# Projections one step sooner, batch loops written out, score rows split around the attend products

## The chip, the cores and the metric

The kernel runs on one core of one Trainium2 chip. The metric is the device time of one execution in microseconds (us). The engines of the core are named as the profile names them: PE (TensorE, with its weight loads as PEld), DVE (VectorE), ACT (ScalarE), POOL (GpSimd) and SP (SyncE, which issues the DMA transfers here). They run side by side, each through its own list of instructions, and meet at semaphores.

## The reference, cut to what matters

Two blocks are computed for x of 4 batches, 512 tokens and 512 columns. The first normalises each token, sends it through one of four experts and adds the gated result. The second, which the change touches, is this for each batch:

```python
def _L0_ffn_ref(hidden_states, ln1_w, ln2_w, Wq, Wk, Wv, Wo, A, B, W_in_base, W_up_base, W_down):
    ...   # H = 16 heads of HD = 32 columns, F_ = 2048, R = 16
    residual = hidden_states
    x = _rmsnorm(hidden_states, ln1_w)
    attn = _attention(x, Wq, Wk, Wv, Wo)      # causal softmax attention
    mod = MOD_SCALE * jnp.tanh(attn @ A)
    h = _rmsnorm(residual, ln2_w)
    gate_pre = h @ W_in_base.T + mod * (h @ A) @ B
    gate = jax.nn.silu(gate_pre)
    up = h @ W_up_base.T
    mlp_out = gate * up @ W_down.T
    return residual + mlp_out
...
x = x + jnp.tanh(g_ffn[0]) * _L0_ffn_ref(_layernorm(x, axis=-1), ...)
```

## The kernel before

All products keep single-precision accuracy by splitting an operand into a high and a low part (fp32r). The high part is an ACT copy, the low part a DVE subtraction, and a product of two split operands is three matmuls. The expert part runs first, to about 161 us. Then the four batches follow, each with an attention stage and an MLP stage of 16 chunks. On every engine but POOL the batches 0 to 2 are one loop (`Fori(0, NB - 1)`, on SP `Fori(1, NB - 1)`) and the last is written behind it.

The attention stage has 16 heads in four groups of four. For each group a Q and a K product (12 matmuls each) go to one PSUM bank, `QKB`, which holds one product at a time: the next may start once ACT has copied the high part (`split_qk`) and DVE has taken the low part (`qk_low`) of the one before. SP loads each head's rows of Q and K into one of two stacks (`load_stack`, three transfers). For head n the steps are then:

- scores (PE, `scores`): four row tiles of 512, 384, 256 and 128 columns, in three banks. The widest one (bank 0) is followed by its causal mask, an added product with the identity; then the 384 and 128 tiles share bank 1 and one mask; then 256 in bank 2 with its mask. Each bank must have been read by the exponentials of the head before.
- maxima (DVE, `maxima`), exponentials (ACT, `exponentials`, four of them, each with its row sum), the reciprocal of the sums (DVE) and the normalisation of the four tiles: `NORM_DVE` tiles 3 and 1 on DVE, `NORM_POOL` tiles 0 and 2 on POOL.
- turn (PE, `turn_probs`): ten transposes of 128x128 into the banks 4, 5 and 6, each of which must be free of the head before; ACT copies the high parts and DVE subtracts the low parts (three each) into `pts`.
- attend (PE, `attend`): eight matmuls against the values, all heads into the one bank `ATT`, which a product with zeros has cleared.

The engines overlap these steps for neighbouring heads. PE's order is written out by hand in `head_step`: in step n it does half a Q or K product if one is due (6 matmuls), the turn of head n+1, the scores of head n+3, the attend products of head n, and in the steps 9 to 14 two matmuls of the first chunk's up product (`up_part`). ACT's step n is the exponentials of n+1, a Q/K copy or a copy of values if due, and the three copies of head n. DVE's step n is reciprocal and normalisation of n+1, a Q/K low part if due, the maxima of n+2, and the three low parts of n. The half products stand in the steps 0 to 8.

## Time and profile before

| | us |
|---|---|
| median of 3 runs | 1061.95 (1060.31 to 1062.95) |
| the profiled execution, its own time | 1061.96 |
| its span (first to last instruction) | 1059.8 |
| PE busy / DVE / ACT / POOL in the span | 1033.5 / 722.4 / 589.6 / 252.1 |

The profiled execution stands for the median: they differ by 0.01 us, and 2.2 us of its time lie around the span. A stage is read by cutting the span where PE changes work. The second batch serves as the example: its opening products begin at 385.40, its first scores at 396.80, the attend products of head 0 at 411.53, of head 7 at 444.23, the first product of the MLP stage at 475.63. The clock of PE is granted in full throughout.

### The profile page before, as it was taken

How to read it: one execution, taken by the hardware profiler on the slowest of the kernel's cores; microseconds unless marked ns; L12 is line 12 of the kernel's file. 1: busy time of each engine (PE TensorE's matmuls, PEld its weight loads, DVE VectorE, ACT ScalarE, POOL GpSimd, SP SyncE). 2: the span in 40 equal slices, each digit the busy share in tenths (PEclk: the TensorE clock that was granted, in tenths of full speed). 3: DMA queues.
4: the chain of work that ended last, by engine and by line, in shares of the span. 5: the costliest groups of instructions: out<-in, count | busy, mean ns of one | idle time of the engine just before them, and what ended most of it. 6: DMA issues, size and time to landing. Idle time of an engine off the chain costs nothing.

```text
span 1059.8 us, 17623 instructions
## 1 busy us (share of the span) xinstructions
PE 1033.5 (98%) x5336; PEld 853.5 (81%) x5337; DVE 722.4 (68%) x1661; ACT 589.6 (56%) x1399; POOL 252.1 (24%) x252
## 2 busy tenths in 40 slices
PE   6999999999999999999999999999999999999998
PEld 6787878877888878878888888778888888788887
DVE  7766756996665559985665479966655599854443
ACT  4464546886434447875444368864344478753342
POOL 4536123641000115640000136410001155300000
PEclk9999999999999999999999999999999999999999
DMA  6534133443222416343322354432234253322221
GB/s 239 201 141 161 49 117 74 96 110 134 90 89 91 147 47 173 69 127 129 106 90 89 111 141 98 113 130 90 89 91 147 63 157 80 95 86 89 89 89 50
DMA packets 47084, 115.93 MB, mean 109 GB/s; under 512 B 6800, under 2 KB 6800, under 8 KB 46096
## 3 DMA queue, kind: packets, MB, share of 16 engines
q1 hardware_dynamic: 43968, 105.06, 33.2%
q0 software_dynamic: 3040, 9.96, 2.7%
q8 instruction: 35, 0.57, 0.2%
q14 instruction: 41, 0.34, 0.1%
HBM read 76.46 MB, written 13.37 MB: 85 GB/s over the span
## 4 chain that ended last, share of the span: by engine, by line
PE 86%; DVE 8%; issue 3%; DMA 1%; ACT 1%; SPq 0%; DVEq 0%; POOL 0%; POOLq 0%
PE bank L518 67%; PE bank L721 5%; PE bank L735 4%; DVE wr L1329 3%; PE bank L684 3%; DVE nb L1341 2%; PE bank L688 1%; PE bank L770 1%; DMA stack<-wr 1%; PE bank L574 1%; PE bank L589 1%; DVE big L1350 1%; PE bank L632 1%; SPq L312 0%; ACT wr L887 0%
## 5 line engine op out<-in xcount | busy, mean ns | idle before, releaser
L518 PE MATMUL bank<-hT,wr 128*128 128x512 f32 x1488 | 358.4, 390 | 0.0
L518 PEld LDWEIGHTS bank<-hT,wr 128*128 128x128 f32 x1488 | 278.8, 188 | 60.0 <-issue 1.3
L518 PE MATMUL bank<-wr,actr 128*128 128x512 f32 (+1 forms) x1224 | 303.1, 397 | 2.4 <-DVE actr L1311 1.5
L518 PEld LDWEIGHTS bank<-wr,actr 128*128 128x128 f32 x1224 | 228.8, 190 | 51.1 <-issue 3.3
L491 POOL TENSOR_SCALAR big<-big,rr 128x128 f32<-128x128 f32 (+1 forms) x128 | 138.9, 1094 | 131.7 <-DVE rr L1346 131.2
L1380 DVE SCALAR_TENSOR_TENSOR wr<-stream,lns,wr 128x256 fp32r<-128x256 f32 x256 | 121.7, 536 | 51.0 <-ACT wr L1006 51.0
L972 ACT ACTIVATE big<-bank,nb 128x512 f32<-128x512 f32 (+3 forms) x256 | 131.7, 527 | 27.9 <-DVE nb L1341 27.7
L430 POOL TENSOR_TENSOR wqs<-wstage,wqs 128x512 fp32r<-128x512 f32 x32 | 43.0, 1353 | 436.8 <-ACT wqs L887 435.4
L1329 DVE TENSOR_TENSOR wr<-bank,wr 128x512 fp32r<-128x512 f32 (+1 forms) x224 | 124.5, 600 | 22.2 <-ACT wr L887 22.2
L887 ACT ACTIVATE wr<-bank 128x512 fp32r<-128x512 f32 (+1 forms) x224 | 106.0, 538 | 52.9 <-PE bank L518 30.1
L887 ACT ACTIVATE actr<-act_sb 128x512 fp32r<-128x512 f32 x64 | 40.4, 632 | 145.7 <-DVE act_sb L1394 145.7
L1018 ACT ACTIVATE sil<-bank 128x512 f32<-128x512 f32 x64 | 38.1, 596 | 137.3 <-PE bank L770 137.3
L1341 DVE TENSOR_REDUCE nb<-bank 128x1 f32<-128x512 f32 (+3 forms) x256 | 107.2, 478 | 3.7 <-PE bank L688 3.0
L1006 ACT ACTIVATE wr<-stream,lns 128x256 fp32r<-128x256 f32 x256 | 108.4, 494 | 0.0
L518 PE MATMUL bank<-hT,wqs 128*128 128x512 f32 x384 | 98.2, 398 | 2.2 <-issue 2.2
L1329 DVE TENSOR_TENSOR wr<-stream,wr 128x512 fp32r<-128x512 f32 x64 | 43.8, 690 | 72.4 <-ACT wr L887 71.7
L721 PE MATMUL bank<-ident,big 128*128 128x128 f32 x640 | 84.9, 276 | 6.0 <-DVE wr L1329 5.0
L721 PEld LDWEIGHTS bank<-ident,big 128*128 128x128 f32 x640 | 71.3, 140 | 23.7 <-DVE wr L1329 14.0
L735 PE MATMUL bank<-wr 128*48 128x512 f32 (+3 forms) x512 | 86.0, 310 | 0.0
L1394 DVE TENSOR_TENSOR act_sb<-bank,sil 128x512 f32<-128x512 f32 x64 | 44.2, 691 | 57.7 <-PE bank L518 51.0
L518 PEld LDWEIGHTS bank<-hT,wqs 128*128 128x128 f32 x384 | 68.8, 188 | 16.3 <-issue 3.9
L735 PEld LDWEIGHTS bank<-wr 128*48 128x48 f32 x512 | 58.2, 122 | 22.9 <-DVE wr L1329 1.8
(180 smaller groups left out, 1039.6 us busy)
## 6 DMA issues: line engine op xcount, KB each, us to landing
stream<-in_wmlp SPq DMA_DIRECT2D x64, 512.0 KB, 4.0
stack<-wr SPq DMA_DIRECT2D x192, 128.0 KB, 2.3
stream<-in_wmlp SPq DMA_DIRECT2D x64, 256.0 KB, 2.7
big<-in_x SPq DMA_DIRECT2D x4, 1024.0 KB
big<-y_rows SPq DMA_DIRECT2D x4, 1024.0 KB, 5.5
residual<-big SPq DMA_DIRECT2D x4, 1024.0 KB
big<-residual SPq DMA_DIRECT2D x4, 1024.0 KB, 5.6
out<-big SPq DMA_DIRECT2D x3, 1024.0 KB, 4.5
```

What stands on the lines that cost most here:

```text
L430: g.tensor_tensor(wqs[:, LO, which, :, :], wqk_v[:, which, :, q * P:q * P + P], wqs[:, HI, which, :, :].bitcast(F32), ALU.subtract).then_i ...
L491: g.tensor_scalar(rows, rows, rr[:, n % 2, qt:qt + 1], None, ALU.mult).then_inc(pn_pool, 1)
L518: mm = pe.matmul(dst, lhs(pl, k), rhs(pr, k), start=start and i == 0, stop=stop and i == n - 1, skip_group_check=skip)
L721: mm = pe.transpose(bank[bk][:, col + (qt - kt) * P:col + (qt - kt) * P + P], prob[par][:, src:src + P], ident[:, :])
L735: mm = pe.matmul(bank[ATT][0:3 * R, kt * P:S], vst[:, q % 2, kt, at_row:at_row + 3 * R], pts[:, j % 2, part, at:at + w], start=False, stop ...
L887: return a.activation(dst, src, ACT.Copy)
L972: a.activation(prob[par][:, at:at + w], bank[bk][:, col:col + w], ACT.Exp, bias=nb[:, qt:qt + 1], accum_out=rs[:, par, qt:qt + 1]).then_in ...
L1006: ins = a.activation(dst[:, :, dt, :], raw[:, :, dt, :], ACT.Copy, scale=lns[:, 1, dt:dt + 1])
L1329: v.tensor_tensor(dst, src, high.bitcast(F32), ALU.subtract).then_inc(done, 1)
L1341: v.reduce_max(nb[:, qt:qt + 1], bank[bk][:, col:col + P * (qt + 1)], AXX, negate=True).then_inc(nb_ok, 1)
L1380: ins = v.scalar_tensor_tensor(out=dst[:, :, dt, :], in0=raw[:, :, dt, :], scalar=lns[:, 1, dt:dt + 1], in1=high[:, :, dt, :].bitcast(F32) ...
L1394: v.tensor_tensor(act_sb[:, :], bank[UP[par]][:, :], sil[:, :], ALU.mult).then_inc(gu_ok, 1)
```

## The change

The Q and K products of the groups 2 and 3 move one step forward: half a product stands at the end of the steps 0 to 6, in front of these one half stands behind the scores of head 2, and the second half of group 1's K product joins the first, ahead of the first turn. So the steps 7 and 8 have none. Their copies (`COPY_AT`) and POOL's weight splits (`WEIGHTS_AT`) move with them. In PE's step n the turn comes first, then the middle and the second bank of the scores of head n+3, then the attend products of head n, then the half product or the up products, then the first (widest) score tile of head n+4. The turn takes the key tiles in another order, and so the three banks are copied smallest first; the attend products wait once for all three banks. Normalisation is shared out anew: tile 3 on DVE, tile 0 on ACT behind its first copy, tiles 1 and 2 on POOL. ACT copies the values ahead of the three copies. The product with zeros is gone, the first attend product starts the bank. The batch loops of PE and SP are written out; those of ACT and DVE stay. The value products use their two banks in the other order.

```diff
-VALUES, LOW_RANK = (4, 6), 5
+VALUES, LOW_RANK = (6, 4), 5
-NORM_DVE, NORM_POOL = (3, 1), (0, 2)
+NORM_DVE, NORM_ACT, NORM_POOL = 3, 0, (1, 2)
+TURN_ORDER = (2, 1, 3, 0)
+TURNED_BANKS = ((6, 256, 1024), (5, 512, 512), (4, 512, 0))
+COPY_AT = {(0, 0): (1, 1), (0, 2): (2, 0), (1, 0): (2, 1), (1, 2): (3, 0), (2, 0): (3, 1)}
+WEIGHTS_AT = {(0, 0): (2, 1), (0, 2): (3, 0), (1, 0): (3, 1)}
+PART_OF = {2: 1, 1: 2, 3: 2, 0: 3}
...
@@ SP: load_stack, batch loop
                     sp.wait_ge(qk_lo, g * 2 + 2)
+                    if q:
+                        sp.wait_ge(s_done, g * (3 * QH) - 3)
...
-            batch(0, True, first=True)
-            with sp.Fori(1, NB - 1) as b:
-                batch(b, True)
-            batch(NB - 1, False)
+            for b in range(NB):
+                batch(b, b < NB - 1, first=b == 0)
...
@@ PE
-            def scores(n, par, loads, first=False):
...
+            def scores_last(n, par, loads, first=False):
                 pe.wait_ge(stk[par], loads)
                 if not first:
                     pe.wait_ge(exp_ok, n * 4 - 3)
+                score_rows(par, 3, True)
                 mask(0, 3 * P, 1)
+            def scores_middle(n, par, first=False):
                 if not first:
                     pe.wait_ge(exp_ok, n * 4 - 1)
+                score_rows(par, 2, True)
+                score_rows(par, 0, False)
                 mask(1, 2 * P, 2)
+            def scores_second(n, par, first=False):
                 if not first:
                     pe.wait_ge(exp_ok, n * 4)
+                score_rows(par, 1, True)
                 mask(2, P, 1)
...
+            def turn_tiles(n, par, kt, first=False):
+                if not first and kt != 3:
+                    pe.wait_ge(pt_lo, (n - 1) * 3 + PART_OF[kt])
+                for qt in range(kt, TT):
+                    turn(n, par, kt, qt)
+            def wait_probs(n):
+                pe.wait_ge(pn_ok, n + 1)
+                pe.wait_ge(pn_act, n + 1)
+                pe.wait_ge(pn_pool, (n + 1) * len(NORM_POOL))
+            def project_part(b, head):
+                q, j = head // QH, head % QH
+                if q < NQ - 2:
+                    project(b, q + 2, j // 2, half=j % 2)
+            def head_step(b, q, j):
+                n = (b * NQ + q) * QH + j
+                head, other = q * QH + j, (j + 1) % 2
...
+                if head < H - 1:
+                    wait_probs(n + 1)
+                    for kt in TURN_ORDER:
+                        turn_tiles(n + 1, other, kt)
+                if head < H - 3:
+                    scores_middle(n + 3, other)
+                    scores_second(n + 3, other)
+                order = (0, 1, 3, 2) if head < H - 1 else TURN_ORDER
+                for i, kt in enumerate(order):
+                    if head == H - 1 and kt != 3:
+                        pe.wait_ge(pt_lo, n * 3 + PART_OF[kt])
+                    elif i == 0:
+                        pe.wait_ge(pt_lo, n * 3 + 3)
+                    attend(kt, HI)
+                    mm = attend(kt, LO)
                 mm.then_inc(pv_done, 1)
                 if head < H - 1:
-                    turn_probs(n + 1, (j + 1) % 2)
...
+                    project_part(b, head + 1)
                 if UP_FROM <= head < H - 1:
...
+                if head < H - 4:
+                    scores_last(n + 4, j % 2, stack_loads(b, head + 4))
...
+                pe.wait_ge(qk_lo, b * (NQ * 2) + 1)
                 values((0, 1))
-                pe.matmul(bank[ATT][:, :], zeror[:, :], hT[:, HI, 0, :], start=True, stop=False,
-                          skip_group_check=True).then_inc(pv_done, 1)
                 pe.wait_ge(qk_lo, b * (NQ * 2) + 2)
+                scores(b * H, 0, stack_loads(b, 0), first=True)
                 project(b, 1, 0)
+                scores(b * H + 1, 1, stack_loads(b, 1))
                 values((2, 3))
+                project(b, 1, 1)
+                wait_probs(b * H)
...
+                scores(b * H + 2, 0, stack_loads(b, 2))
+                project_part(b, 0)
+                scores_last(b * H + 3, 1, stack_loads(b, 3))
...
-            with pe.Fori(0, NB - 1) as b:
-                batch(b, True)
-            batch(NB - 1, False)
+            for b in range(NB):
+                batch(b, b < NB - 1)
@@ ACT
+            def normalise(n, par):
+                act.wait_ge(rr_ok, n + 1)
+                rows = prob_rows(par, NORM_ACT)
+                a.activation(rows, rows, ACT.Copy, scale=rr[:, par, NORM_ACT:NORM_ACT + 1]).then_inc(pn_act, 1)
...
+                for i, (bk, w, at) in enumerate(TURNED_BANKS):
+                    act.wait_ge(p_turned, n * 3 + i + 1)
+                    copy(pts[:, j % 2, HI, at:at + w], bank[bk][:, 0:w]).then_inc(pt_hi, 1)
+                    if i == 0 and (q < NQ - 1 or j < QH - 1):
+                        normalise(n + 1, (j + 1) % 2)
...
@@ DVE
-                for qt in NORM_DVE:
-                    rows = prob_rows(par, qt)
-                    v.tensor_scalar(rows, rows, rr[:, par, qt:qt + 1], None, ALU.mult).then_inc(pn_ok, 1)
+                rows = prob_rows(par, NORM_DVE)
+                v.tensor_scalar(rows, rows, rr[:, par, NORM_DVE:NORM_DVE + 1], None, ALU.mult).then_inc(pn_ok, 1)
...
```

## Rows read from the trace of the kernel before

**Rows 1.** The page: busy time and share of the span, per engine.
```profile
PE 1033.5 (98%) x5336; PEld 853.5 (81%) x5337; DVE 722.4 (68%) x1661; ACT 589.6 (56%) x1399; POOL 252.1 (24%) x252
```

**Rows 2.** Windows of the second batch's attention stage: start:end, length, each engine's busy us.
```profile
396.80:411.53 14.73, 14.73 (x97) 13.38 (x97) 13.98 (x37) 11.57 (x36) 7.59 (x8) 1.00 0.74 216
444.23:475.63 31.40, 29.96 (x198) 22.62 (x197) 29.49 (x70) 24.79 (x73) 13.88 (x13) 1.00 0.37 95
444.23:448.88 4.65, 4.65 (x33) 3.97 (x33) 4.62 (x12) 3.98 (x12) 2.56 (x3) 1.00 0.00 0
461.94:466.09 4.15, 4.10 (x29) 3.11 (x29) 4.12 (x11) 3.62 (x11) 2.18 (x3) 1.00 0.69 244
```

**Rows 3.** Timeline of PE: start, us, line, operation; one step with half a product.
```profile
444.23 1.34 PE L735 MATMUL bank<-wr 128*48 128x512 f32 x8
445.41 1.60 PE L518 MATMUL bank<-hT,wqs 128*128 128x512 f32 x6
446.85 1.25 PE L721 MATMUL bank<-ident,big 128*128 128x128 f32 x10
447.86 0.47 PE L684 MATMUL bank<-stack 96*128 96x512 f32 x1
...
448.23 0.45 PE L684 MATMUL bank<-stack 96*128 96x384 f32 x2
...
```

**Rows 4.** Timeline of PE: turns of later heads; idle time before one, and its releaser.
```profile
450.82 1.47 PE L721 MATMUL bank<-ident,big 128*128 128x128 f32 x10 [0.60 <-DVE wr L1329]
...
463.84 1.47 PE L721 MATMUL bank<-ident,big 128*128 128x128 f32 x10
```

**Rows 5.** Timeline of DVE: a reciprocal with products about, then one later step.
```profile
442.66 0.16 DVE L1346 RECIPROCAL rr<-rs 128x4 f32<-128x4 f32 x1
...
460.49 0.16 DVE L1346 RECIPROCAL rr<-rs 128x4 f32<-128x4 f32 x1
460.69 0.86 DVE L1350 TENSOR_SCALAR big<-big,rr 128x512 f32<-128x512 f32 x2
461.50 1.68 DVE L1341 TENSOR_REDUCE nb<-bank 128x1 f32<-128x512 f32 x4
463.10 1.61 DVE L1329 TENSOR_TENSOR wr<-bank,wr 128x512 fp32r<-128x512 f32 x3
```

**Rows 6.** Timeline of ACT, one later step: first and last exponential piece, copies.
```profile
462.23 0.69 ACT L972 ACTIVATE big<-bank,nb 128x512 f32<-128x512 f32 x1 [0.37 <-DVE nb L1341]
...
464.16 0.21 ACT L972 ACTIVATION_READ_ACCUMULATOR big<-bank,nb 128x1 f32 x1
464.53 1.47 ACT L887 ACTIVATE wr<-bank 128x512 fp32r<-128x512 f32 x3 [0.16 <-PE bank L721]
```

**Rows 7.** Groups by shape: count, busy us, mean ns of one, idle before.
```profile
L491 POOL TENSOR_SCALAR big<-big,rr 128x384 f32<-128x384 f32 x64 | 79.5, 1242 | 0.0
L491 POOL TENSOR_SCALAR big<-big,rr 128x128 f32<-128x128 f32 x64 | 60.6, 947 | 131.7 <-DVE rr L1346 131.2
...
L1350 DVE TENSOR_SCALAR big<-big,rr 128x512 f32<-128x512 f32 x64 | 31.1, 486 | 2.3
...
L972 ACT ACTIVATE big<-bank,nb 128x128 f32<-128x128 f32 x64 | 23.4, 366 | 0.0
...
L887 ACT ACTIVATE wr<-bank 128x512 fp32r<-128x512 f32 x160 | 88.3, 597 | 52.9 <-PE bank L518 30.1 <-PE bank L721 19.7 <-DMA stack<-wr 3.1
```

**Rows 8.** Windows over the seams of batches 0/1, 1/2, 2/3: same work, three times.
```profile
381.70:391.62 9.92, 8.85 (x39) 6.69 (x38) 4.71 (x7) 3.12 (x7) 0.00 (x0) 1.00 0.03 8
606.79:616.74 9.95, 8.84 (x40) 6.69 (x37) 4.71 (x7) 3.12 (x7) 0.00 (x0) 1.00 0.03 8
832.07:840.33 8.26, 8.26 (x39) 6.85 (x38) 4.70 (x7) 3.13 (x7) 0.00 (x0) 1.00 0.01 3
```

**Rows 9.** Timeline of PE: behind the first seam, and a batch's first scores.
```profile
171.72 0.50 PE L684 MATMUL bank<-stack 96*128 96x512 f32 x1 [0.26 <-DMA stack<-wr]
...
385.40 2.56 PE L518 MATMUL bank<-hT,wqs 128*128 128x512 f32 x10 [0.72 <-issue]
```

More of the change, by code:

```diff
@@ L745, in head_step, with attend @@
[L745 to L748 removed]
+                head, other = q * QH + j, (j + 1) % 2
+                def attend(kt, part):
+                    _, _, at = TURNED[kt]
+                    at_row = 64 * (j // 2) + R * (j % 2)
+                    return pe.matmul(bank[ATT][0:3 * R, kt * P:S], vst[:, q % 2, kt, at_row:at_row + 3 * R],
+                                     pts[:, j % 2, part, at:at + S - kt * P], start=head == 0 and kt == 0 and part == HI, stop=False,
+                                     skip_group_check=True)
```

111 lines of the change are left out of this document (43 added, 68 removed).

## The prediction, made before the changed kernel had run

> **What bounds the kernel now.** The page comes first: PE is busy for 98% of the span [rows 1]. That seems to leave 26 us, but busy is not the same as useful, so the stage that the change touches is cut into windows next. In the second batch the attention stage, from its first scores at 396.80 to the MLP stage at 475.63, has two different halves. While half products are in the steps, PE is busy without a gap, 4.65 us a step [rows 2]. In the later steps, such as the one from 461.94, DVE is busy for 4.12 of 4.15 us, and PE does not need that long [rows 2]. What PE needs is read from starts on its timeline [rows 3]: attend 445.41 - 444.23 = 1.18, half product 446.85 - 445.41 = 1.44 (six matmuls of 512 columns, 0.24 each), turn 447.86 - 446.85 = 1.01, widest score tile with mask 0.37, the other score tiles 448.88 - 448.23 = 0.65. Together 4.65, the whole step. Without the half product it is 3.21, with two up matmuls (0.48) 3.69; the rest of the later steps' 4.15 is DVE's pace. The trace says so too: the turn at 450.82 comes 0.60 late because of DVE, and the turn, 1.25 long in a full step, is drawn out to 1.47 there [rows 3, 4]. DVE's own step is reciprocal to next reciprocal: 0.20 + 0.81 + 1.60 + 1.53 = 4.14 by its starts [rows 5]. A third loss lies between the batches: the same opening work takes 9.92 and 9.95 us where the batch loop of PE jumps back, and 8.26 us at the last batch, which is entered without a jump [rows 8]. PE stands there with nothing to wait for (0.72 at 385.40 put down to issue [rows 9]).
>
> **The seams.** Writing PE's loop out makes the first two seams like the third: 9.92 + 9.95 - 2 x 8.26 = 3.35 us gained, with no loss elsewhere that the trace suggests, since the straight code behind the third seam runs without gaps. Loops of ACT and DVE stay, but both wait for PE at the seam. From the trace alone the gain lies between 0 (PE must fetch the same instructions either way, rival 2) and 3.35; I take 3.3.
>
> **The opening up to the first attend.** It took 396.80 to 411.53, 14.73 us, all busy [rows 2]. One half product more stands here: +1.44. The turn of head 1 follows sooner behind the scores of head 2, whose maxima DVE has to do before the low parts of head 0; laid out from the durations of rows 3 to 7, PE waits 0.3 there (0 to 0.5). Sum +1.7 a batch. The product with zeros (0.24) gives nothing: the first scores behind it wait for the stack's load [rows 9], and that load starts when K is split, which is not moved. The weights (POOL), the copies of Q and K and the stacks of this part all end before PE wants them, by 0.6 us or more in the same layout; SP's added wait asks for scores that are done one step before.
>
> **The steps with half products.** From the attend of head 0 to that of head 7 the stage took 444.23 - 411.53 = 32.70 [rows 2]; seven steps of 4.65 are 32.55, so 0.2 of small waits goes. What changes inside a step are neighbours. The trace shows 0.07 us of excess where the 512 tile and its mask (640 columns, 0.30 at the pace of the half product) follow the turn, 0.37 [rows 3]; that tile now follows a half product. In exchange a turn now follows a 128-column mask, which the trace of before never shows, and the 384 tile follows the turn. I take 0 for the exchange; bounds -0.10 (the excess is all lost with the old neighbours) and +0.05 a step (it moves to the new ones and the mask hides less of the turn's first weights). Over 12 steps and 4 batches: -4.8 to +2.4 us.
>
> **The steps without.** From the attend of head 7 to the MLP stage the stage took 31.40, PE idle for 1.44 of it and stretched for more [rows 2]. PE's own work there is after the change: 2 x 3.21 (steps 7 and 8 have no filler), 3 x 3.69, 2 x 2.66 (attend, up, turn, no scores left), 1.66, and the last attend 1.20: 25.7. Whether PE reaches that is decided by the others. DVE loses one normalisation of 256 columns: the pair takes 0.86, the 512 tile alone 0.49 [rows 5, 7], so 4.14 - 0.38 = 3.76 a step. ACT's step was 464.37 - 462.23 = 2.14 for the exponentials and 1.36 to 1.47 for the copies [rows 6]; it gains a normalisation of 128 columns. No such ACT row exists; the exponential of 128 columns takes 0.37 [rows 7], and overlapped starts cost about 0.1 less, so I take 0.25 (bounds 0.2 and 0.6, the latter if it also waits for the reciprocal, which DVE issues after the exponentials and its own low parts). ACT's step is then 3.80. POOL's two tiles are 256 and 384 columns where they were 128 and 384: 0.95 and 1.24 [rows 7] give 1.10 for 256 on the straight line, 2.34 in sum, far below 3.8, but it stands between reciprocal and turn.
>
> So ACT and DVE do a step in 3.8, PE in 3.2 to 3.7, and PE lives on a **lead** that the others have built: turn of a head minus its reciprocal. It was 446.85 - 442.66 = 4.2 with products about and 463.84 - 460.49 = 3.35 where DVE binds [rows 3 to 5]. After the change the others need some 4.15 in a full step (3.8, plus a Q/K part every other step, a value copy every fourth), PE 4.65, so the lead grows by 0.5 a step up to what the scores allow: the reciprocal of head n+2 comes at least 1.65 of PE work (turn and two score groups) and about 1.3 (last maximum, last exponential, hand-over) behind the start of the turn of n, so the lead is at most 2 x 4.65 - 2.95 = 6.35. I take 5.9 at head 8. From the turn of head 8 to that of 15 PE needs 23.5 (2 x 3.21 + 3 x 3.69 + 3.3 + 2.7), the reciprocals 7 x 3.8 + 0.85 (one Q/K part, one value part) = 27.5, and the last turn can't start before its reciprocal plus 2.65 (POOL's 2.34 and two hand-overs). PE waits 27.5 + 2.65 - 23.5 - 5.9 = 0.75, bounds 0 and 2.5 (a lead of 4.2). So 25.7 + 0.7 = 26.4 in place of 31.4: -5.0 a batch.
>
> POOL's tiles can be counted in another way. The 128-column tile takes 0.95 and one three times as wide 1.24 [rows 7], so some of the first is waiting beside DVE's normalisation, which starts with it. The Trainium skill ("SBUF — State Buffer", section "Who interferes with whom") says that a VectorE `tensor_scalar` in a two-port mode takes a port pair which GpSimd shares, and that the second to come is blocked until the first ends. By that rule the columns alone would cost 1.24/384 x 256 = 0.83 and the wait 0.43 behind a shorter DVE operation, 2.5 in place of 2.34 for both, and the sum below would be 0.6 us higher.
>
> **The sum.** A batch: +1.7 - 0.2 - 5.0 = -3.5. Four batches and the seams: -14.0 - 3.3 = -17.3. Against the profiled execution's 1061.96, which stands for the median of 1061.95, that is 1044.7. The MLP stages, where PE is the bound, and the expert part are untouched. Unknowns: exchange of neighbours -4.8 to +2.4, waits at the end of the stage -3.0 to +7.2, wait at head 1 -1.2 to +0.8: from 1036 to 1055.
>
> **Rivals.** (1) *ACT takes DVE's place*, 15%. If the normalisation in front of ACT's last two copies costs 0.55 or more with its wait, ACT's step is 4.14 again, DVE's old pace. Then the lead stays at 4.2, the reciprocals take 29.8, and PE waits 29.8 + 2.65 - 23.5 - 4.2 = 4.75 a batch: 4.0 worse than the forecast, a batch no longer gains, and with the seams 1044.7 + 16.0 = 1060.7 is left. For it: ACT is strictly in order and the reciprocal is waited for in the middle of its copies. Against: ACT had 0.53 us idle a step where DVE was the bound [rows 6], and the reciprocal follows the exponentials within 0.3.
>
> (2) *The written-out loop doesn't do what it says*: the seam is instruction fetch that straight code pays elsewhere, 15%. Then 1044.7 + 3.3 = 1048.0. Against it stands the third seam.
>
> (3) *The bank of Q and K becomes the new wait*, 8%, the side where it gets slower. Half products stand directly behind the attend products now, and the first half of each product waits until ACT (0.60 [rows 7]) and DVE (about as much) have split the one before, which they do behind the exponentials and the normalisation of the next step. By my layout the split is done about 1 us ahead of PE at the step with the smallest lead, and later by more. If it came after PE by w at the three products of a batch that start in the steps 1, 3 and 5, it would cost 12 w, and behind it on PE stand the next score tile and the next turn. From w = 1.45 it eats the whole gain; if the split falls one set of exponentials further back (w = 2.3 by 2.14 of rows 6), the time is 1044.7 + 27.6 = 1072.3. For it: before, the copies had a full step more. Against: a wait on PE gives the others lead, so that it should not repeat.
>
> **How the numbers follow.** Forecast 62%, rivals 15, 15 and 8%. A measurement of this kernel can tell about 0.3% (3.2 us) from no change. Faster by more: the forecast, rival 2 and a third of rival 1, 82%. Within: two thirds of rival 1 and the mild end of rival 3, 12%. Slower: 6%. The forecast's own range is 1036 to 1055; rival 2 lies in it, and with it the range holds a little under 8 in 10, so it reaches to 1057, into rival 1.
>
> **What would show it.** Right: no issue gaps at the three seams; steps of heads 1 to 7 at 4.65; the steps behind at 3.2 to 3.7 with PE idle under 1 us a batch; DVE idle for 5 to 10% there; the attend of head 0 about 1.7 later behind the first scores. Wrong: later steps at 4.1 with ACT without a gap (rival 1), a gap in front of half products released by DVE (rival 3), issue gaps inside the stage (rival 2), full steps of 4.7 or more (the exchange of neighbours). A stack that lands late, or POOL, would show as the releaser of the turn or of the widest tile.

## The result, and the profile after

The changed kernel takes **1054.3 us** (median, 1053.1 to 1055.7) where the kernel before takes 1061.35 (1060.3 to 1063.0) beside it: a ratio of 0.9927, 95% interval 0.9914 to 0.9940. The spans of the two profiled executions are 1053.2 and 1059.8 us. So it is 7 us faster; the forecast was 17 us.

The windows answer to [rows 2, 8]: the first two seams between batches, and in the second batch the opening (first scores to the attend of head 0), the steps with half products (to the attend of head 7) and the later steps (to the MLP stage). After start:end come the length, then the busy us of PE, PEld, DVE, ACT and POOL, the clock, DMA share and GB/s.

```profile
381.25:389.51 8.26, 8.26 (x39) 6.85 (x38) 4.71 (x7) 3.13 (x7) 0.00 (x0) 1.00 0.01 4
394.78:412.15 17.37, 16.17 (x102) 14.34 (x103) 13.50 (x33) 11.96 (x39) 10.19 (x10) 1.00 0.72 205
412.15:443.93 31.78, 31.78 (x220) 27.39 (x219) 29.53 (x69) 28.46 (x91) 20.94 (x19) 1.00 0.39 88
443.93:472.52 28.59, 27.93 (x191) 21.15 (x191) 26.64 (x63) 25.25 (x79) 15.36 (x13) 1.00 0.40 102
603.59:611.85 8.26, 8.26 (x40) 6.85 (x39) 4.71 (x7) 3.13 (x7) 0.00 (x0) 1.00 0.02 6
```

Against the forecast, per batch: opening 17.37 - 14.73 = **+2.64** (forecast +1.7), steps with half products 31.78 - 32.70 = **-0.92** (-0.2), later steps 28.59 - 31.40 = **-2.81** (-5.0). Together -1.09 where -3.5 was forecast. The seams give 9.92 + 9.95 - 2 x 8.26 = 3.35, as forecast. With four batches that is 7.7, near the 6.6 and 7.05 of spans and medians. The second batch stands for the others: by PE's timeline the later steps of the four are 28.59, 28.59, 28.94 and 28.57 (one step of the third is 0.34 longer), the other stretches agree within 0.02.

PE's timeline shows the opening's loss: the turn of head 1 starts 1.20 late, put down to a low part of DVE. Behind the dots stand an attend near the end of the batch (L764) and the last turn of the batch, which comes 0.52 late for POOL.

```profile
408.99 0.23 PE L692 MATMUL bank<-maskr,identr 128*128 128x128 f32 x1
410.42 1.31 PE L727 MATMUL bank<-ident,big 128*128 128x128 f32 x10 [1.20 <-DVE wr L1374]
...
466.19 1.42 PE L764 MATMUL bank<-wr 128*48 128x512 f32 x8
468.60 1.28 PE L727 MATMUL bank<-ident,big 128*128 128x128 f32 x10 [0.52 <-POOL big L497]
```

DVE's timeline names the low part (409.95, taken from SBUF, not from a bank: it is that of the values). It also shows a step with half products that has a hole in front of the maxima (439.40) and a later step that has none (446.49 to 450.26: 0.20 + 0.41 + 1.64 + 1.52 = 3.77; 4.14 before, [rows 5]).

```profile
409.95 0.41 DVE L1374 TENSOR_TENSOR wr<-big,wr 128x256 fp32r<-128x256 f32 x1
...
437.87 0.17 DVE L1391 RECIPROCAL rr<-rs 128x4 f32<-128x4 f32 x1
...
439.40 1.09 DVE L1386 TENSOR_REDUCE nb<-bank 128x1 f32<-128x384 f32 x3 [0.24 <-PE bank L692]
...
446.49 0.17 DVE L1391 RECIPROCAL rr<-rs 128x4 f32<-128x4 f32 x1
446.69 0.48 DVE L1394 TENSOR_SCALAR big<-big,rr 128x512 f32<-128x512 f32 x1
447.10 1.73 DVE L1386 TENSOR_REDUCE nb<-bank 128x1 f32<-128x512 f32 x4
448.74 1.61 DVE L1374 TENSOR_TENSOR wr<-bank,wr 128x256 fp32r<-128x256 f32 x3
450.26 0.17 DVE L1391 RECIPROCAL rr<-rs 128x4 f32<-128x4 f32 x1
```

The lead of head 8 (start of its turn on PE minus its reciprocal on DVE) is 442.23 - 437.87 = 4.36, where the forecast had 5.9. In front of that turn the widest score tile and its mask now take 0.30 (0.37 in [rows 3]).

```profile
441.93 0.39 PE L688 MATMUL bank<-stack 96*128 96x512 f32 x1
442.17 0.22 PE L692 MATMUL bank<-maskr,identr 128*128 128x128 f32 x1
442.23 1.26 PE L727 MATMUL bank<-ident,big 128*128 128x128 f32 x10
```

The groups by shape, to be held against [rows 7] (count, busy us, mean ns of one, idle before):

```profile
L497 POOL TENSOR_SCALAR big<-big,rr 128x384 f32<-128x384 f32 x64 | 79.5, 1242 | 0.0
L497 POOL TENSOR_SCALAR big<-big,rr 128x256 f32<-128x256 f32 x64 | 77.9, 1217 | 112.0 <-DVE rr L1391 112.0
...
L1017 ACT ACTIVATE big<-big,rr 128x128 f32<-128x128 f32 x64 | 25.5, 399 | 2.2 <-DVE rr L1391 1.3
```

### The profile page after: what moved, and what is told of

The parts are those of the page before. It is cut to its first block, busy times and chain, and to the rows that moved or that the text cites. A ratio compares the mean times of both kernels' runs of the same rounds, so it can differ in the third digit from the quotient of the medians.

```text
span 1053.2 us, 17255 instructions
## 1 busy us (share of the span) xinstructions
PE 1024.6 (97%) x5332; PEld 849.2 (81%) x5333; DVE 701.5 (67%) x1597; ACT 601.0 (57%) x1463; POOL 269.7 (26%) x252
## 4 chain that ended last, share of the span: by engine, by line
PE 82%; DVE 9%; issue 2%; DMA 2%; POOL 2%; ACT 1%; SPq 1%; DVEq 0%; POOLq 0%
PE bank L525 67%; PE bank L727 4%; DVE wr L1374 4%; PE bank L764 4%; DVE nb L1386 3%; PE bank L688 2%; PE bank L804 1%; DMA stack<-wr 1%; PE bank L692 1%; POOL big L497 1%; DMA big<-in_x,gidx 1%; PE bank L581 1%; PE bank L596 1%; PE bank L639 1%; SPq L320 1%
## 5 line engine op out<-in xcount | busy, mean ns | idle before, releaser
L497 POOL TENSOR_SCALAR big<-big,rr 128x256 f32<-128x256 f32 (+1 forms) x128 | 156.3, 1230 | 112.0 <-DVE rr L1391 112.0
L926 ACT ACTIVATE wr<-bank 128x512 fp32r<-128x512 f32 (+1 forms) x224 | 112.6, 537 | 55.8 <-PE bank L525 35.6
L1386 DVE TENSOR_REDUCE nb<-bank 128x1 f32<-128x512 f32 (+3 forms) x256 | 109.7, 483 | 7.9 <-PE bank L692 7.5
L525 PE MATMUL bank<-hT,wqs 128*128 128x512 f32 x384 | 95.9, 393 | 0.0
L727 PE MATMUL bank<-ident,big 128*128 128x128 f32 x640 | 87.5, 277 | 7.3 <-DVE wr L1374 4.8
L727 PEld LDWEIGHTS bank<-ident,big 128*128 128x128 f32 x640 | 68.4, 141 | 22.5 <-DVE wr L1374 12.5
L764 PE MATMUL bank<-wr 128*48 128x512 f32 (+3 forms) x512 | 85.5, 309 | 0.0
L688 PE MATMUL bank<-stack 96*128 96x512 f32 (+3 forms) x256 | 74.3, 335 | 2.6 <-DMA stack<-wr 2.6
```

Of the source, the lines that this page charges most:

```text
L497: g.tensor_scalar(rows, rows, rr[:, n % 2, qt:qt + 1], None, ALU.mult).then_inc(pn_pool, 1)
L525: mm = pe.matmul(dst, lhs(pl, k), rhs(pr, k), start=start and i == 0, stop=stop and i == n - 1, skip_group_check=skip)
L688: pe.matmul(bank[bk][:, col:col + w], stack[:, par, 0, qt * P:qt * P + P], stack[:, par, 1, 0:w], start=start, stop=False, skip_group_chec ...
L727: mm = pe.transpose(bank[bk][:, col + (qt - kt) * P:col + (qt - kt) * P + P], prob[par][:, src:src + P], ident[:, :])
L764: return pe.matmul(bank[ATT][0:3 * R, kt * P:S], vst[:, q % 2, kt, at_row:at_row + 3 * R], pts[:, j % 2, part, at:at + S - kt * P], start= ...
L926: return a.activation(dst, src, ACT.Copy)
```

## The experiments

All are edits of the changed kernel, or of its first improvement ("value wait"), except the run of the old kernel with its loops written out. The three last columns are the lengths of the three stretches of the second batch in each profile, read as above; they say where a gain or loss lies. Kernels that ran at different times are compared by their ratios.

| kernel | median us | ratio to before, 95% | opening | with half products | later steps |
|---|---|---|---|---|---|
| before | 1061.35 | | 14.73 | 32.70 | 31.40 |
| changed | 1054.30 | 0.9927 (0.9914 to 0.9940) | 17.37 | 31.78 | 28.59 |
| value wait at the attend | 1050.65 | 0.9898 (0.9882 to 0.9913) | 16.38 | 31.78 | 28.64 |
| scores ahead of the turn | 1056.81 | 0.9956 (0.9943 to 0.9970) | 17.37 | 32.16 | 28.85 |
| scores in one piece | 1066.18 | 1.0044 (1.0030 to 1.0058) | 17.72 | 32.19 | 30.82 |
| before, loops written out | 1057.21 | 0.9958 (0.9944 to 0.9972) | 14.67 | 32.64 | 31.16 |
| old shares | 1059.82 | 0.9985 (0.9976 to 0.9994) | 17.36 | 31.79 | 30.01 |
| two zero matmuls a half product | 1066.22 | 1.0041 (1.0027 to 1.0055) | 17.37 | 34.93 | 28.59 |
| value wait, POOL 512 and 384 | 1054.01 | 0.9930 (0.9918 to 0.9943) | 16.36 | 31.84 | 29.47 |
| value wait, POOL 512, 384, 128 | 1060.26 | 0.9992 (0.9982 to 1.0002) | 16.38 | 32.40 | 30.75 |
| value wait, DVE's tile cut | 1048.82 | 0.9877 (0.9860 to 0.9893) | 16.38 | 31.77 | 28.19 |
| ... and ACT's left out | 1048.08 | 0.9868 (0.9852 to 0.9885) | 16.35 | 31.78 | 28.02 |
| value wait, POOL's tiles cut | 1047.51 | 0.9866 (0.9849 to 0.9882) | 16.37 | 31.78 | 27.86 |
| value wait, last K's low part cut | 1049.45 | 0.9884 (0.9867 to 0.9900) | 16.37 | 31.77 | 28.56 |
| DVE's, ACT's and a low part cut | 1044.72 | 0.9831 (0.9815 to 0.9848) | 16.38 | 31.77 | 26.93 |
| value wait, zeros behind the turn | 1056.45 | 0.9946 (0.9929 to 0.9962) | 16.34 | 32.12 | 30.05 |
| value wait, last head to DVE | 1046.98 | 0.9865 (0.9846 to 0.9883) | 16.36 | 31.78 | 27.84 |

**The value wait.** In the changed `head_step` of PE the wait for the values' low part stands ahead of the next head's turn; only the attend products need it. (The cut diff ahead of the prediction leaves these two lines out; in the kernel before, the wait stood in front of the attend products.)

```diff
-                if j == 0:
-                    pe.wait_ge(vst_lo, b * NQ + q + 1)
                 if head < H - 1:
                     wait_probs(n + 1)
 ...
+                if j == 0:
+                    pe.wait_ge(vst_lo, b * NQ + q + 1)
                 for i, kt in enumerate(order):
```

> The changed kernel with one wait moved: in the steps 0, 4, 8 and 12 PE's wait for the low part of the values stands in front of the attend products again instead of in front of the turn. Theory V (the 1.20 us that PE idles before the turn of head 1 is this wait, since the low part of the values ends at 410.36 and the turn starts at 410.42): the turn of head 1 starts about 1.0 us earlier behind the first scores, the attend of head 0 too, and the time falls by 2.5 to 4.4 us, to 1050 to 1052 beside the changed kernel's 1054.3. Rival (the wait is for the low parts of head 0, as the prediction had it): the idle time stays near 1.2 and the time at 1054.

Theory V holds: 3.65 us less, 0.99 a batch, all in the opening. In PE's timeline the turn of head 1 follows the widest tile's mask without a wait (drawn out to 1.69, as it waits for low parts within), and the attend comes 16.38 behind the first scores: 14.73 + 1.65, where the forecast had 14.73 + 1.7.

```profile
408.21 0.22 PE L692 MATMUL bank<-maskr,identr 128*128 128x128 f32 x1
408.27 1.69 PE L727 MATMUL bank<-ident,big 128*128 128x128 f32 x10
...
410.38 1.33 PE L764 MATMUL bank<-wr 128*48 128x512 f32 x8
```

**Scores ahead of the turn.** If DVE's hole in front of the maxima is what caps the lead, scores that come sooner should lift it.

```diff
+                if 0 < head < 7:
+                    scores_middle(n + 3, other)
+                    scores_second(n + 3, other)
                 if head < H - 1:
                     wait_probs(n + 1)
 ...
-                if head < H - 3:
+                if head == 0 or 7 <= head < H - 3:
                     scores_middle(n + 3, other)
                     scores_second(n + 3, other)
```

> The changed kernel with PE's order changed in the steps 1 to 6: the second and third score group of head n+3 stand in front of the turn of head n+1. Theory L (the lead of the others over PE is capped at about 4.8 us, because DVE takes these maxima, then the low parts, then the next reciprocal, and so the reciprocal of head n+2 comes 4.2 us behind the start of the turn of head n): the maxima come 1.0 us earlier in PE's step, DVE idles less before them, the lead at the turn of head 8 grows from 4.4 by 0.8 to 1.4, PE waits about 1 us less from head 8 on, and the time falls by 2 to 5 us, to 1049 to 1052. Rival P (ACT and DVE are simply as slow as PE in the full steps): lead and time stay, 1054, or get worse as PE waits for exponentials.

It missed: 2.5 slower than the changed kernel, the lead at head 8 still 443.34 - 438.96 = 4.38. The turn now stands later in PE's step, and ACT, which copies what the turn makes ahead of the next exponentials, waits for it (the waits between 412 and 445: us in total, times, longest). DVE's hole went from the maxima (0.6 of such waits are left, 1.7 in the changed kernel) to the reciprocal.

```profile
ACT wr L929 <- PE bank L727: 3.2, 4, 0.9
DVE rr L1394 <- ACT big L1014: 2.5, 4, 0.8
```

**Scores in one piece.** The widest score tile goes back behind the turn.

```diff
                 if head < H - 3:
+                    scores_last(n + 3, other, stack_loads(b, head + 3))
                     scores_middle(n + 3, other)
 ...
-                if head < H - 4:
-                    scores_last(n + 4, j % 2, stack_loads(b, head + 4))
 ...
-                scores_last(b * H + 3, 1, stack_loads(b, 3))
```

> The changed kernel with the widest score tile of head n+3 back behind the turn, in one piece with the other score tiles, instead of at the end of the step before. Theory N (the full step is 4.54 instead of 4.65 us because the widest tile follows a half product and no longer the turn): full steps are 4.64 to 4.65 again, 0.7 us a batch more between the attends of head 0 and head 7, and with the maxima that come later the time rises by 3 to 6 us, to 1057 to 1060. Rival (the neighbours have nothing to do with it): full steps stay at 4.54 and the time within 1.5 us of 1054.3.

It cost 11.9, far more than either theory had, and makes the kernel slower than before. The steps with half products are 4.60, a loss of 0.06; most of it, 2.2 of 3.0 a batch, lies in the later steps, which are 4.25 where they were 3.77. DVE can't begin its maxima: it waits 0.43 for the mask in front of them. (By starts: low parts over at 462.69, maxima 1.12 later, low parts 1.60 after that, over 1.53 later; together the 4.25.)

```profile
462.69 0.16 DVE L1389 RECIPROCAL rr<-rs 128x4 f32<-128x4 f32 x1
462.89 0.48 DVE L1392 TENSOR_SCALAR big<-big,rr 128x512 f32<-128x512 f32 x1
463.81 1.68 DVE L1384 TENSOR_REDUCE nb<-bank 128x1 f32<-128x512 f32 x4 [0.43 <-PE bank L692]
465.41 1.61 DVE L1372 TENSOR_TENSOR wr<-bank,wr 128x256 fp32r<-128x256 f32 x3
466.94 0.17 DVE L1389 RECIPROCAL rr<-rs 128x4 f32<-128x4 f32 x1
```

**Only the loops.** The kernel before with the batch loops of PE and SP written out.

```diff
 ...
-            with pe.Fori(0, NB - 1) as b:
-                batch(b, True)
-            batch(NB - 1, False)
+            for b in range(NB):
+                batch(b, b < NB - 1)
```

> The kernel before with the batch loops of PE and SP written out and nothing else changed. If the seams cost what the windows over them show, 9.92 and 9.95 in place of 8.26, the time falls by 3.3 us, to 1058.0 beside 1061.35, and nothing else in the trace moves. Rival 2 of the prediction (straight code pays for its fetch elsewhere): 1061.

4.0 us less, so more than half of what the whole change brings. Behind the last down products PE goes on without the 0.72 and 0.35 of issue that it had; from 382.06 to 390.32 it takes the 8.26 of the straight seam. The seams are 3.35 of the 4.0; the later steps of the second batch also take 0.24 less (31.16 for 31.40), so some of the changed kernel's 2.81 there may be the loop's and not the new order's; no run separates them. The loops of PE and SP were written out together, so the run doesn't tell them apart.

```profile
382.06 2.98 PE L516 MATMUL bank<-wr,actr 128*128 128x512 f32 x12
384.88 5.60 PE L516 MATMUL bank<-hT,wqs 128*128 128x512 f32 x24
390.32 1.98 PE L822 MATMUL bank<-hT,apad 128*128 128x512 f32 x8
```

**Old shares.** The normalisation divided as before.

```diff
-NORM_DVE, NORM_ACT, NORM_POOL = 3, 0, (1, 2)
+NORM_DVE, NORM_POOL = (3, 1), (0, 2)
 ...
```

> The changed kernel with the normalisation divided as in the kernel before: VectorE the tiles of 512 and 256 columns, GpSimd those of 128 and 384, ScalarE none. The changed kernel took 1054.3; its later steps are 3.77 long, VectorE busy for 3.73 to 3.75 of it and ScalarE for 3.71 to 3.77. Theory (VectorE and ScalarE both set the pace of the later steps, and the division moved it from 4.14 to 3.77): the later steps go back to about 4.1, seven of them, so +2.3 us a batch, 1063 (1060 to 1065), with ScalarE idle for some 0.3 a step. Rival (ScalarE sets the later steps; VectorE's share is covered): the steps stay at 3.75 or less and the time at 1053 to 1056.

5.5 us more, just under the theory's range (by 0.2) and far from the rival: behind the last half product the attends follow each other in 3.96, 4.09 and 4.11, and the later steps lose 1.42 a batch. The new division is worth about that, not more.

**More lead.** Two matmuls against zeros in each half product make every full step longer for PE and for nobody else: by 0.48 by their columns, by 0.45 as measured.

```diff
+                if half == 1:
+                    for k in range(2):
+                        pe.matmul(bank[to][:, :], zeror[:, :], hT[:, HI, k, :], start=False, stop=False,
+                                  skip_group_check=True)
 ...
```

> The changed kernel with two more matmuls of 512 columns against zeros in each half product, 0.24 each, so 0.48 more in every full step and in the opening: 8 a batch, 3.84 us a batch, +15.4 in four. What is asked is how the lead (turn of a head minus its reciprocal, 4.36 to 4.85 in the changed kernel, 4.36 at head 8) answers to longer full steps. Theory L (the reciprocal of head n+2 can only come some 4.2 to 4.7 behind the turn of n, so the lead is two steps less that): the lead grows by 2 x 0.48 = 0.96 within two steps and then stands still, 5.3 at head 8, and the steps without half products take 0.9 less: 1054.3 + 15.4 - 3.6 = 1066 (1064.5 to 1067.5). Theory P (VectorE and ScalarE just need as long as TensorE in a full step, no cap): the lead grows by 0.48 at every full step, to about 7, until TensorE no longer waits behind them: 1057 to 1062. Third (the lead doesn't answer): 1069 to 1070.

The total is theory L's, 1066.2, but not for its reason. The lead does what L said: 449.46 - 444.21 = 5.25 at head 8, and between 5.2 and 5.75 from the second step on, so it is capped. Yet the later steps take 28.59, to the hundredth what they take with 0.9 less lead. The saving came elsewhere: 0.48 a batch in the opening, where the value wait covered the added work, and 0.03 a step (the stretches give 12.6 in four batches, the medians 11.9). **A larger lead at head 8 buys nothing.** With that L falls as an explanation of the time, and so does the forecast's use of the lead. (The first two lines are from DVE's and PE's timelines, the others are windows.)

```profile
444.21 0.17 DVE L1399 RECIPROCAL rr<-rs 128x4 f32<-128x4 f32 x1
...
449.46 1.26 PE L735 MATMUL bank<-ident,big 128*128 128x128 f32 x10
...
398.84:416.21 17.37, 16.59 (x104) 14.80 (x105) 13.49 (x33) 11.94 (x39) 10.18 (x10) 1.00 0.70 205
416.21:451.14 34.93, 34.93 (x233) 29.95 (x233) 29.57 (x69) 28.38 (x91) 21.34 (x19) 1.00 0.35 80
451.14:479.73 28.59, 27.91 (x192) 21.23 (x192) 26.65 (x63) 25.25 (x79) 14.89 (x13) 1.00 0.39 103
```

**Tiles to POOL.** Two divisions that take work from DVE, then from DVE and ACT (the first is shown; the second also gives POOL tile 0, as its last).

```diff
-NORM_DVE, NORM_ACT, NORM_POOL = 3, 0, (1, 2)
+NORM_DVE, NORM_ACT, NORM_POOL = 1, 0, (3, 2)
 ...
```

> The version with the value wait in front of the attend products (1050.65, 3.65 faster than the changed kernel), and VectorE and GpSimd exchange tiles: VectorE normalises the 256 columns, GpSimd the 512 and the 384, ScalarE the 128 as before. VectorE's step becomes 3.76 - 0.19 = 3.57; GpSimd's two tiles become about 2.7 in place of 2.44; ScalarE's 3.71 to 3.77 stays. Theory (VectorE and ScalarE are both at their limit in the later steps): ScalarE alone holds the pace at 3.72 or more, nothing is gained: 1049.5 to 1051.5, VectorE idle for about 0.2 a step. Rival (VectorE alone sets the pace, ScalarE only looks busy because it waits within its copies): 3.57 a step, 7 x 0.19 x 4 = 5.3 less, 1045 to 1046.

> As the run beside it with the exchange of the 512 and 256 tiles, and ScalarE's 128 columns go to GpSimd too, as the last of its three tiles. VectorE's step is 3.57, ScalarE's about 3.5, GpSimd's three tiles some 3.3 to 3.6, which is less than the 4.3 that the low parts need behind the reciprocal. Theory (VectorE and ScalarE both at their limit): now both are relieved, the later steps go to 3.57: 7 x 0.19 x 4 = 5.3 less than 1050.65, less what the last turn of a batch waits longer for GpSimd (0.7 x 4 = 2.8): 1048 (1046 to 1049.5). Rival (GpSimd becomes the last one ahead of the turn): steps of 3.8 and more, 1051 to 1056.

Both missed on the slow side, by 3.4 and 9.6 against the version with the value wait. POOL's 512 columns take 1.71, so the pair takes 2.94, the three 3.53, and the turn starts 3.46 and 3.89 behind its reciprocal in place of 2.96: POOL has room in its own time, but it stands between reciprocal and turn. That closes a loop over two heads: the reciprocal of head n+2 comes some 4.26 behind the turn of n (442.23 to 446.49 in the changed kernel), and its turn POOL's time later. With 3.46 that is 7.72, and two steps of the exchange run take 3.77 + 3.96 = 7.73; with 3.89 it is 8.15, and two steps take 3.77 + 4.38 = 8.15. In the changed kernel it is 7.22, less than its two steps (7.54), so there something else binds. These runs therefore don't show whether DVE's step alone sets the pace; the next ones take work away and give it to nobody.

```profile
449.43 2.94 POOL L497 TENSOR_SCALAR big<-big,rr 128x512 f32<-128x512 f32 x2 [0.82 <-DVE rr L1391]
```

**Work left out.** DVE's tile cut to 128 columns, then also ACT's tile left out; POOL's tiles cut; the last K's low part cut.

```diff
-                rows = prob_rows(par, NORM_DVE)
+                rows = prob_rows(par, NORM_DVE)[:, 0:P]
 ...
```

```diff
-                    rows = prob_rows(n % 2, qt)
+                    rows = prob_rows(n % 2, qt)[:, 0:P]
```

```diff
+                cols = 16 if (q, which) == (NQ - 1, 1) else S
+                low(qk[:, q % 2, (Q_LO, K_LO)[which], 0:cols], bank[at][:, 0:cols], qk[:, q % 2, (Q_HI, K_HI)[which], 0:cols], qk_lo)
```

> The version with the value wait in front of the attend products (1050.65). VectorE normalises 128 of the 512 columns of its tile and leaves the other 384 as they are, so that its step in the part without half products gets 0.49 - 0.2 = 0.3 shorter, with nothing given to another engine. The version's steps there are 3.77 long, VectorE 3.73 to 3.75 busy, ScalarE 3.71 to 3.77. Theory (both at their limit): ScalarE holds the pace, at most 0.06 a step is gained over 7 steps and 4 batches: 1049 (1048 to 1050.7), VectorE idle for 0.3 a step. Rival (VectorE alone sets the pace): 3.47 a step, 0.3 x 7 x 4 = 8.4 less: 1042 (1041 to 1044).

> As the run beside it, and ScalarE's tile of 128 columns is not normalised at all: 0.28 less a step on ScalarE, 0.3 less on VectorE. Theory (both at their limit, nothing else near): the steps without half products go to 3.5: 0.27 x 7 x 4 = 7.6 less, 1043 (1042 to 1044.5). Rival (the loop over two heads is as tight: reciprocal to turn 2.96 by GpSimd's two tiles, turn to the reciprocal two heads later 4.2 at least, together 7.2 in two steps): 3.6 a step, 0.17 x 7 x 4 = 4.8 less, 1046 (1044.5 to 1047.5).

> The version with the value wait in front of the attend products (1050.65). GpSimd normalises 128 columns of each of its two tiles and leaves the rest as it is: 2.44 becomes some 1.5, and the turn can start 2.1 behind its reciprocal in place of 2.96. Theory (VectorE and ScalarE at their limit): the steps without half products stay at 3.77, and only the last turn of a batch comes sooner, by the 0.5 that it waits for GpSimd, up to 0.8: 1050.65 - 2 to 3 = 1048 (1047 to 1049). Rival (GpSimd's time stands in the loop that sets the pace): two steps take 0.85 less, 0.4 x 7 x 4 = 11 less: 1040 (1038 to 1044).

> The version with the value wait in front of the attend products (1050.65). Of the last K (group 3) VectorE makes the low part of 16 columns only, the other 496 keep what group 1 left. In the changed kernel VectorE starts this low part 0.5 behind the turn of head 8, when the last half product and ScalarE's copy of it are done, and from there to the last turn of the batch it has no gap: 0.61, then maxima 1.59, low parts 1.53, the reciprocal of head 10, and five steps of 3.77. Theory (the end of the last half product and VectorE's work behind it set the part without half products, whatever lead there was): 0.5 less a batch, 1050.65 - 2.0 = 1048.6 (1048 to 1049.2). Rival (the copies and exponentials of ScalarE, in order behind the same half product, are as late): 1050 to 1051.

The cut on DVE alone gives 1.8 us, as expected of two engines at their limit; by the stages it is 0.45 a batch in the later steps, none of it in the steps of heads 7 to 9. With ACT's tile left out as well, 1043 or 1046 was expected; it is 1048.1, only 0.7 below the run before. POOL's cut gives 3.1, 0.71 a batch of it at the last turn. The last K's low part gives 0.1 a batch in the later steps, so what lies behind the last half product is not the reason either; the 1.2 us between the medians is not clear of the noise (the two intervals overlap). In all four the intervals from the attends of heads 7, 8 and 9 to the next stay at 3.77 to 3.79. So neither DVE, ACT nor POOL alone, nor DVE and ACT together, holds the 3.77. The run with DVE and ACT relieved shows what does: DVE now has time, and waits 0.15 for PE's mask in the middle of its maxima,

```profile
445.97 1.61 DVE L1365 TENSOR_TENSOR wr<-bank,wr 128x256 fp32r<-128x256 f32 x3
447.49 0.17 DVE L1382 RECIPROCAL rr<-rs 128x4 f32<-128x4 f32 x1
...
448.74 1.09 DVE L1377 TENSOR_REDUCE nb<-bank 128x1 f32<-128x384 f32 x3 [0.15 <-PE bank L692]
449.74 1.61 DVE L1365 TENSOR_TENSOR wr<-bank,wr 128x256 fp32r<-128x256 f32 x3
451.27 0.41 DVE L1365 TENSOR_TENSOR wr<-big,wr 128x256 fp32r<-128x256 f32 x1
```

while the turn on PE waits for DVE's low parts (waits between the attends of heads 8 and 10: us in total, times, longest).

```profile
PEld bank L727 <- DVE wr L1365: 0.7, 3, 0.3
DVE nb L1377 <- PE bank L692: 0.3, 2, 0.2
```

That is a **loop of one head**. The last low part of head m frees the bank for the last tile of the turn of m+1; behind the turn stand the second and third score groups; behind their masks DVE's last three maxima; behind these, in DVE's order, the low parts of m+1. By starts in this run, where each operation begins as the one before it ends: low parts over at 447.49, last three maxima from 448.74 (1.25 later, spent on PE), low parts from 449.74 (1.00), over at 451.27 (1.53). That is 3.78. In the changed kernel DVE's own operations fill the same 3.77, ACT is busy for as much, and PE needs 3.61 where it has up matmuls (read below, where it has no gap): four limits within 0.2.

**The loop made shorter and longer.** One run leaves out part of the last low part (on top of the two cuts), one puts matmuls against zeros between turn and scores, in steps where PE has time to spare.

```diff
+                    cols = P if q * QH + j >= 7 and i == 2 else w
 ...
```

```diff
+                for k in range(more):
+                    pe.matmul(bank[1][:, 0:3 * P], zeror[:, :], hT[:, HI, k, 0:3 * P], start=True, stop=False,
+                              skip_group_check=True)
 ...
```

> The run with VectorE's tile cut to 128 columns and ScalarE's left out (1048.08; its attend intervals behind the last half product are still 3.78, 3.78, 3.77, though VectorE then needs 3.53 and ScalarE 3.5), and from head 7 on the third low part of a head takes 128 columns in place of 512 (the other 384 keep what an earlier head left). Theory (a loop of one head between TensorE and VectorE: the last low part frees the bank of the turn's last tile, behind the turn stand the second and third score groups, behind these the maxima, behind these the next low parts; 3.77 by its own length): the loop gets 0.4 shorter, the steps of heads 7 and 8 go to about 3.5, where ScalarE stands, those with two up matmuls to TensorE's own 3.69: 0.3 + 0.3 + 3 x 0.08 + up to 0.4 at the end, 4 to 5 in four batches: 1043.5 (1042.5 to 1045). Rival (something else holds the steps at 3.77): 1047 to 1048.5.

> The version with the value wait in front of the attend products (1050.65), and in the steps of heads 7 to 12 two matmuls of 384 columns against zeros between the turn and the second score group, 0.16 each by columns, 0.32 a step on TensorE. In the steps of heads 7 and 8 TensorE needs 3.21 of 3.77 on its own, in the others 3.69. Theory (the loop of one head runs through TensorE behind the turn): every one of the six steps gets 0.32 longer, also those of heads 7 and 8, 4.1 in place of 3.77: 7.7 in four batches: 1058.3 (1056.5 to 1059.5). Rival (VectorE's or ScalarE's occupancy holds 3.77, and TensorE has 0.56 to spare in two of the steps): heads 7 and 8 stay at 3.77 to 3.8, the other four get 0.24 longer: 3.8 in four batches: 1054.5 (1053.5 to 1055.5).

The loop holds both ways. Shorter by 0.4, the intervals behind the attends of heads 7 to 11 are 3.60 to 3.63, and the later steps get 1.09 a batch shorter. Why they don't reach 3.5 can be read from the trace. From head 9 to head 12 PE is busy without a gap, 3.61 a step, so there it is the limit itself. At heads 7 and 8 the bank that comes last is another: the turn (here that of head 9) now waits for the second low part, which was not cut. PE's weight load stands 0.33 in front of the third transpose, and the eight from there on follow each other.

```profile
440.91 0.86 PEld L727 LDWEIGHTS bank<-ident,big 128*128 128x128 f32 x8 [0.33 <-DVE wr L1365]
...
446.04:456.88 10.84, 10.84 (x83) 9.43 (x83) 10.08 (x28) 10.53 (x34) 6.72 (x8) 1.00 0.63 170
```

In the other run the loop is longer by some 0.34 (0.32 was estimated), and the intervals behind the attends of heads 7 and 8 go from 3.78 to 4.12, although PE had 0.56 to spare there. A PE that only waited for DVE's or ACT's occupancy would have hidden it, and so would the loop over two heads: 7.22 + 0.34 in two steps is 3.78 a step.

```profile
442.10 1.33 PE L767 MATMUL bank<-wr 128*48 128x512 f32 x8
...
446.22 1.32 PE L767 MATMUL bank<-wr 128*48 128x512 f32 x8
...
450.34 1.33 PE L767 MATMUL bank<-wr 128*48 128x512 f32 x8
```

The stretches got 0.34 + 1.41 = 1.75 a batch longer, 7.0 in four; the median only 5.8, between the two expectations; where the other 1.2 went isn't shown. The steps decide, not the sum: the rival would have left those of heads 7 and 8 as they were.

**The last head to DVE.** DVE has no maxima at the last head, so it takes POOL's second tile there.

```diff
+                if last:
+                    rows = prob_rows(par, NORM_POOL[1])
+                    v.tensor_scalar(rows, rows, rr[:, par, NORM_POOL[1]:NORM_POOL[1] + 1], None, ALU.mult)
 ...
```

> The version with the value wait in front of the attend products (1050.65, ratio 0.990 to the kernel before), and at the last head of a batch VectorE normalises the tiles of 384 and 512 columns, GpSimd only that of 256; VectorE has no maxima left to do there. The last turn of a batch came 2.96 behind its reciprocal, 0.52 of it waiting for GpSimd, and the low parts of the head before come 0.4 later by the second tile on VectorE. Theory (GpSimd's second tile is the last thing in front of this turn, VectorE's low parts of the head before end 2.5 behind the reciprocal): 0.4 to 0.9 less a batch: 1050.65 - 2.5 = 1048.2 (1047 to 1049.2). Rival (the low parts of the head before, later by 0.4, are as late for the turn's tiles): 1050 to 1051.

0.80 a batch, 3.7 in all: the last turn starts 463.46 - 461.19 = 2.27 behind its reciprocal (2.96 before) and waits for nothing. This version, **1046.98 us, ratio 0.9865 (0.9846 to 0.9883)**, beats both kernels.

## Why the prediction was wrong

**What bounds it** was read rightly: PE with half products in the steps, DVE in the later ones, a loop's jump at the seams. The seams gave 3.35 and the written-out loops alone 4.0, so rival 2 is refuted.

**The opening** failed by a wait. The working laid out the order of the products and the maxima, but not the wait for the values' low part, which the change moves ahead of the next turn. The term of the sum that it spoils is the 0.3 (bounds 0 and 0.5) for the turn of head 1: PE idled 1.20 there, and the stretch came out 0.94 over its +1.7. With the wait at the attends it is +1.65. The prediction weighs SP's added wait and the bank of Q and K; this wait, moved within PE's own list, is not among them.

**The steps with half products** failed by the value chosen between two bounds: the exchange of neighbours was taken as 0, bounds -0.10 and +0.05; it came out as 4.65 - 4.54 = 0.11 less a step, just outside. By starts the widest tile and its mask take 0.07 less, and the turn takes 1.01 with its new neighbours as with the old. With the widest tile back behind the turn 0.06 of it was lost again; the rest wasn't tested.

**The later steps** hold the step that failed: "PE lives on a lead". The engines' own times were sized about right. DVE's step was forecast at 3.76 and is 3.77; ACT's normalisation at 0.25 and costs 0.29 to 0.31 by starts; POOL's pair at 2.34 and takes 2.46 by its means, nearer to the 2.5 of the rule weighed there (the Trainium skill, "SBUF — State Buffer", section "Who interferes with whom"). From these the forecast let reciprocals run at 3.8 a step, and PE at 3.21 to 3.69 on a stock of 5.9. Two things are wrong with it. The stock is capped lower, 4.36 at head 8. The last maximum of head n+2 comes behind PE's scores, and behind it, in DVE's order, another 1.53 of low parts stand in front of the reciprocal. The cap of 6.35 left these out: it had the reciprocal 2.95 behind the turn two heads before, and it is 4.26. And a stock doesn't help at all, as the run with 5.25 shows: PE's turn needs not only the reciprocal of its head but a bank, which the low parts of the head before free, and those stand behind maxima of scores that PE issues behind its turn. So PE can't run ahead of DVE by a step, whatever the lead. From attend to attend, heads 7 and 8 take 3.79 and 3.77 instead of 3.21, 1.14 a batch. Head 10 takes 4.06, with a value part in DVE's order, 0.37 over. Behind heads 12 and 13 (3.09 and 3.45 instead of 2.66 each) the turns stand 2.96 behind their reciprocals, POOL's tiles between: 1.2. Together, with 0.2 of smaller ones, 2.9 over PE's own 25.7, where 0.75 was forecast: 2.2 a batch, 8.8 us in four. The missed wait adds 3.8, the better neighbours take back 2.9; that makes the 9.6 us between forecast and median, within 0.1.

**The rivals** didn't happen. ACT didn't take DVE's place: relieving it, on top of DVE, gave less than 1 us. No half product waited for the bank of Q and K: PE's list of waits in the changed kernel has none there. The measured time lies in the range, near the end that a lead of 4.2 gave it; that bound was the right size for a wrong reason.

## What to carry over

A lead is worth time only if nothing else ties the two engines: before counting on it, follow every resource, the banks too, from one step to the next, and add up the loop that it closes. When a wait moves in an in-order queue, ask what now stands behind it, even if its owner needs it anyway; moved behind the turn, this one was worth half as much as the whole change. And judge an experiment by the stretch that it aims at, as a right total can have a wrong reason.

## What the hardware showed that was not expected

POOL's first tile behind a reciprocal takes longer than its columns explain. The groups by shape of the run with three tiles on POOL, taken in the order 512, 384, 128:

```profile
L497 POOL TENSOR_SCALAR big<-big,rr 128x512 f32<-128x512 f32 x64 | 109.4, 1709 | 51.2 <-DVE rr L1382 50.5
L497 POOL TENSOR_SCALAR big<-big,rr 128x384 f32<-128x384 f32 x64 | 79.5, 1242 | 0.0
L497 POOL TENSOR_SCALAR big<-big,rr 128x128 f32<-128x128 f32 x64 | 38.5, 602 | 0.0
```

In last place 128 columns take 0.60, in second 384 take 1.24. On that line 256 would take 0.92 and 512 would take 1.56. In first place, where DVE's normalisation starts at the same reciprocal, 512 take 1.71 beside DVE's 256, 256 take 1.22 beside DVE's 512, and 128 took 0.95 beside DVE's pair [rows 7]: 0.15, 0.30 and 0.35 more. In the run with DVE's tile cut to 128 columns POOL's first 256 take 1.02, 0.10 more. So in these runs POOL's first tile takes longer, the longer DVE's operation beside it is. The Trainium skill ("SBUF — State Buffer", section "Who interferes with whom") says that a `tensor_scalar` of VectorE in a two-port mode shuts GpSimd out of a shared port pair until it ends; these numbers agree in direction, but the 0.30 beside 512 columns is less than the 0.43 that the prediction worked out from that rule. No run here has POOL's first tile without DVE beside it.

A jump back of the batch loops costs 1.66 and 1.69 us of PE's time at the two seams ([rows 8] against the windows after). At the first, PE's timeline shows 0.72 and 0.35 of it as issue, time in which PE waits for nothing that the profile shows. SP's loop jumped back too, and no run has only one of them written out.
